# First attention of a graph network on one Trainium2 core: products three steps behind, one 138-column matmul for projection, scores and router

## The reference

```python
# first layer, attention (x: 8 x 1024 x 128, adj: 8 x 1024 x 1024 int32)
h = matmul(layernorm(x), W)
f1 = einsum('bnf,f->bn', h, a1); f2 = einsum('bnf,f->bn', h, a2)
e = leaky_relu(f1[:, :, None] + f2[:, None, :], negative_slope=0.2)
attention = softmax(where(adj > 0, e, -9e15), axis=1)
x = x + elu(matmul(attention, h))
# first layer, router of the experts (8 experts, 2 chosen)
z = layernorm(x)
mu, var = mean(z), mean(square(z - mu))
xn = (z - mu) * rsqrt(var + eps) * gamma + beta
logits = einsum('bsd,de->bse', xn, Wr) + br
top_vals, top_idx = top_k(logits, 2)        # softmax of these two are the shares
# then: experts on xn, second attention, second mixture of experts
```

## Time and profile before

| | |
|---|---|
| median of 3 runs | 1481.67 us (1479.19 to 1484.16) |
| the profiled execution's own time | 1483.64 us |
| its span, first to last instruction | 1481.9 us |
| TensorE busy | 1228.5 us, 83% |
| ScalarE, VectorE, GpSimd busy | 762.9, 655.1, 455.2 us |
| mean granted TensorE clock | 0.874 |
| product of the first attention (L539) | 256 rows, 168.1 us |
| `relu` (L631) waited for the logits | 114.9 us |

### The profile page before, as it was taken

How to read it: one execution, slowest core, us unless ns; L and a number is a source line. 1 busy time by engine, 2 the same in 40 slices (tenths; PEclk the granted TensorE clock), 3 DMA queues, 4 the chain that set the end, 5 groups by cost and what they waited for, 6 DMA issues and landing times. The chain is left out here.

```text
span 1481.9 us, 19195 instructions
## 1 busy us (share of the span) xinstructions
PE 1228.5 (83%) x5480; PEld 743.4 (50%) x5512; DVE 655.1 (44%) x2079; ACT 762.9 (51%) x1077; POOL 455.2 (31%) x519
## 2 busy tenths in 40 slices
PE   4988889788850899934687897799968999999998
PEld 3445445344430677722465675577754444444443
DVE  5565655656453233322454554465433422222222
ACT  4764663566530455512454464466643566656665
POOL 5133564553476112147414523532113200000000
PEclk8887787789775899976788998999985999999999
DMA  8832542441212344442212212211100000000000
GB/s 283 294 142 102 195 140 98 160 162 50 84 40 100 110 136 130 135 136 59 64 49 58 70 54 56 67 56 56 51 0 0 8 15 7 14 14 14 7 14 21
DMA packets 75543, 120.48 MB, mean 81 GB/s; under 512 B 8862, under 2 KB 49676, under 8 KB 74444
## 3 DMA queue, kind: packets, MB, share of 16 engines
q1 hardware_dynamic: 64156, 92.56, 19.1%
q0 software_dynamic: 11312, 27.02, 5.9%
HBM read 77.60 MB, written 41.94 MB: 81 GB/s over the span
## 5 line engine op out<-in xcount | busy, mean ns | idle before, releaser
L2097 DVE TENSOR_TENSOR dGW<-H,WBC 128x512 f32<-128x512 f32 x128 | 98.7, 771 | 231.6 <-ACT H L2065 230.8
L539 PE MATMUL O<-Y,HS 128*128 128x512 f32 x256 | 168.1, 792 | 15.0 <-DVE HS L790 14.9
L1746 DVE CUSTOM_DVE_ANT_0 f_Y<-f_T,f_R 128x1024 f32<-128x1024 f32 x64 | 78.4, 1225 | 197.3 <-ACT f_R L1699 160.8
L2065 ACT ACTIVATE H<-eU,bn 128x512 f32<-128x512 f32 x128 | 99.5, 777 | 114.9 <-PE eU L2009 114.8
L397 POOL DMA_INDIRECT sorted_x<-V,AT_I x128 | 124.6, 974 | 102.3 <-DVE AT_I L839 64.4
L1658 PEld LDWEIGHTS f_O<-f_XN,f_PT 128*128 128x128 f32 x1024 | 137.6, 211 | 35.9 <-issue 17.9
L1634 PE MATMUL f_T<-f_XT,f_XTA 128*128 128x512 f32 x256 | 137.7, 616 | 20.1 <-issue 13.7
L1658 PE MATMUL f_O<-f_XN,f_PT 128*128 128x128 f32 x1024 | 139.9, 295 | 12.4 <-ACT f_PT L1713 12.1
L631 ACT ACTIVATE R<-T,F 128x1024 f32<-128x1024 f32 x64 | 71.0, 1110 | 145.5 <-PE T L526 114.9
L1580 POOL DMA_INDIRECT W<-sorted_y,ROW_I x128 | 122.2, 955 | 42.8 <-issue 42.8
L2003 PE MATMUL eU<-XTN,V 128*128 (+1 forms) x256 | 132.5, 600 | 1.1 <-PEq L1879 1.1
(11 more groups left out here) (230 smaller groups left out, 1975.0 us busy)
## 6 DMA issues: line engine op xcount, KB each, us to landing
ADJ<-in_adj SPq DMA_DIRECT2D x64, 512.0 KB, 4.5
masks<-NM SPq DMA_DIRECT2D x8, 2048.0 KB
f_MK<-masks SPq DMA_DIRECT2D x64, 256.0 KB
XB<-sorted_x SPq DMA_DIRECT2D x39, 256.0 KB, 2.8
sorted_y<-YB POOLq DMA_DIRECT2D x39, 256.0 KB, 2.7
X<-in_x SPq DMA_DIRECT2D x8, 512.0 KB, 8.1
out_x<-X SPq DMA_DIRECT2D x16, 256.0 KB, 2.3
sorted_x<-zero SPq DMA_DIRECT2D x9, 256.0 KB
```

What stands on the lines that cost most here:

```text
L539: i = pe.matmul(O[:, h * HALF:(h + 1) * HALF], HS[:, g % 2, :], Y[:, g % 3, h * HALF:(h + 1) * HALF], start=False, stop=(c == NT - 1))
L1746: v.tensor_tensor_reduce(Y[:, g % 3, :], T[g % 2][:, :], R4[:, g % 2, :], -SLOPE, 3.0e38, ALU.add, ALU.min, LOW[:, g % RING:g % RING + 1]) ...
L2065: nc.scalar.activation(H2[:, s % 2, :], U2[s % 2][:, :], ACT.Relu, bias=bn[:, 3 * E + e:3 * E + e + 1], scale=bn[:, 2 * E + e:2 * E + e + ...
L2097: nc.vector.tensor_tensor(GW[:, s % 2, :], H2[:, s % 2, :], WBC[:, e, q * HALF:(q + 1) * HALF], ALU.mult).then_inc(gw_ready, 1)
```

## The change

- **One matmul for three results.** Wg is widened from 128 to 138 columns: the projection's weights, the two score vectors, and the router's weights scaled by gamma. `project` writes a tile's 138 columns, in three pieces of 3, 3 and 2 tiles (a PSUM bank holds three), and H keeps them all. `scores` is gone.
- **The router without transposes of its own.** The mean over features is taken out of the router's weights beforehand. The router is linear, so that its logits are the sum of two parts: that of the layer's input, which comes from the ten added columns times the row's deviation (XG), and that of the attention's ELU, a matmul with the transposes' source EL, which lies in SBUF already. `turn_r` and `copy_xr` are gone, `route` reads EL, and `choose` adds XG, multiplies by the root of the second norm (ROOT_R) and adds the bias.
- **Products three steps behind**, with Y in 4 buffers instead of 3, HS in 3 instead of 2.
- **Places of the extras.** `route` and `choose` of a sample stand at steps 5 and 7 of the next one, not at step 0 of the one after that; `rank` and `seat` at step 0, not 3; on TensorE an extra stands between a step's logits and its product, not behind the product. On GpSimd all 16 sends of a sample are one block ahead of the norms.
- Four loads more in the first stage (router weights, bias, gamma, beta), and two small matmuls ahead of the first transposes.

```diff
-        Wg = sb("Wg", [P, P])
-        WgT = sb("WgT", [P, 2])
+        WIDE = P + 2 + E
+        Wg = sb("Wg", [P, WIDE])
+        gb = sb("gb", [P, 2])
...
-                dve.wait_ge(gat_loaded, 32)
+                dve.wait_ge(gat_loaded, 96)
+                nc.vector.tensor_scalar(Wg[:, P + 2:WIDE], Wr0[:, :], gb[:, 0:1], None, ALU.mult).then_inc(gat_loaded, 1)
                 for k in range(2):
-                    nc.vector.tensor_tensor_reduce(products[:, :], Wg[:, :], A12[:, k * P:(k + 1) * P], 1.0, 0.0, ALU.mult,
-                                                   ALU.add, WgT[:, k:k + 1]).then_inc(gat_loaded, 1)
-                    dve.wait_ge(gat_loaded, 33 + k)
+                    nc.vector.tensor_tensor_reduce(products[:, :], Wg[:, 0:P], A12[:, k * P:(k + 1) * P], 1.0, 0.0, ALU.mult,
+                                                   ALU.add, Wg[:, P + k:P + k + 1]).then_inc(gat_loaded, 1)
+                    dve.wait_ge(gat_loaded, 98 + k)
...
+            THIRD = [(0, 3), (3, 6), (6, 8)]
+            MH = [M[0], M[1], M[0]]
...
-                def project(b, h):
-                    pe.wait_ge(xnt_ready[h], b + 1)
-                    for t in range(4 * h, 4 * h + 4):
-                        i = pe.matmul(M[h][:, t % 4 * P:(t % 4 + 1) * P], XNT[:, t * P:(t + 1) * P], Wg[:, :], start=True, stop=True)
-                    i.then_inc(h_ps[h], 1)
-
-                def scores(b):
-                    pe.wait_ge(h_ready[1], b + 1)
-                    for t in range(NT):
-                        i = pe.matmul(M[1][:, 2 * t:2 * t + 2], XNT[:, t * P:(t + 1) * P], WgT[:, :], start=True, stop=True)
-                    i.then_inc(f12_ps, 1)
+                def project(b, k):
+                    pe.wait_ge(xnt_ready[k > 0], b + 1)
+                    if k == 0:
+                        pe.wait_ge(xnt_ready[1], b + 1)
+                    elif k == 2:
+                        pe.wait_ge(h_ready[0], b + 1)
+                    first, end = THIRD[k]
+                    for t in range(first, end):
+                        i = pe.matmul(MH[k][:, (t - first) * WIDE:(t - first + 1) * WIDE], XNT[:, t * P:(t + 1) * P], Wg[:, :],
+                                      start=True, stop=True)
+                    i.then_inc(h_ps[k], 1)
...
                 def route(b):
-                    for h in range(2):
-                        pe.wait_ge(xrt_ready[h], b + 1)
+                    pe.wait_ge(x_added[0], b + 1)
                     for t in range(NT):
-                        i = pe.matmul(M[0][:, t * E:(t + 1) * E], XRT[:, t * P:(t + 1) * P], Wr0[:, :], start=True, stop=True)
+                        i = pe.matmul(M[0][:, t * E:(t + 1) * E], EL[:, t * P:(t + 1) * P], Wg[:, P + 2:WIDE], start=True, stop=True)
                     i.then_inc(lg_ps, 1)
...
+                pe.wait_ge(g_ready, 2)
+                pe.matmul(M[0][:, 0:E], XNT[:, 0:P], Wg[:, P + 2:WIDE], start=True, stop=True)
+                pe.matmul(M[0][:, E:2 * E], XNT[:, P:2 * P], Wr0[:, :], start=True, stop=True).then_inc(g_ps, 1)
+                pe.wait_ge(g_ready, 3)
...
+                for k in range(3):
+                    project(0, k)
                 turn_f1(0)
                 for g in range(G):
                     b, c = g // NT, g % NT
                     logits(g)
-                    if g >= 2:
-                        attend(g - 2)
                     if c == 0 and b >= 2:
-                        route(b - 2)
+                        pe.wait_ge(before_ready, 1)
+                        rank(b - 2)
                     if c == 1 and b < LAST:
                         for h in range(2):
                             turn_x(b + 1, h)
                     if c == 2 and b < LAST:
-                        for h in range(2):
-                            project(b + 1, h)
-                    if c == 3 and b >= 2:
-                        pe.wait_ge(before_ready, 1)
-                        rank(b - 2)
+                        for k in range(2):
+                            project(b + 1, k)
                     if c == 3 and b < LAST:
-                        scores(b + 1)
+                        project(b + 1, 2)
                     if c == 4 and b >= 1:
                         for h in range(2):
                             turn_el(b - 1, h)
                     if c == 5 and b < LAST:
                         turn_f1(b + 1)
-                    if c == 6 and b == 1:
-                        pe.wait_ge(x_added[0], 1)
+                    if c == 5 and b >= 1:
+                        route(b - 1)
+                    if c == 7 and b == 1:
+                        pe.wait_ge(f1r_ready, 3)
                         pe.wait_ge(par_loaded, 16 * len(loads))
-                        pe.transpose(M[0][:, 0:R], prow[:, :], ident[0:R, 0:R]).then_inc(pcol_ps, 1)
-                    if c == 7 and b >= 1:
-                        for h in range(2):
-                            turn_r(b - 1, h)
-                attend(G - 2)
-                route(LAST - 1)
-                attend(G - 1)
+                        pe.transpose(M[1][:, 0:R], prow[:, :], ident[0:R, 0:R]).then_inc(pcol_ps, 1)
+                    if g >= 3:
+                        attend(g - 3)
                 rank(LAST - 1)
+                for g in range(G - 3, G):
...
-                    if c == 0 and b >= 2:
-                        for h in range(2):
-                            copy_xr(b - 2, h)
+                    if c == 3 and b >= 1:
+                        grown(b - 1)
                     relu(g)
                     if g >= 1:
                         prob(g - 1)
-                    if c == 1 and b >= 1:
-                        grown(b - 1)
-                    if c == 2 and b < LAST:
+                    if c == 0 and b >= 2:
+                        weight(b - 2)
+                    if c == 0 and b >= 1:
+                        look(b, 3)
+                    if c == 1 and b < LAST:
                         for h in range(2):
                             copy_xnt(b + 1, h)
+                    if c == 2 and b < LAST:
+                        for k in range(2):
+                            copy_h(b + 1, k)
                     if c == 3 and b < LAST:
-                        for h in range(2):
-                            copy_h(b + 1, h)
-                    if c == 3 and b >= 2:
-                        weight(b - 2)
-                    if c >= 4 and b < LAST:
-                        look(b + 1, c - 4)
-                for h in range(2):
-                    copy_xr(LAST - 1, h)
+                        copy_h(b + 1, 2)
+                    if c in (4, 5, 7) and b < LAST:
+                        look(b + 1, (4, 5, 7).index(c))
...
-                    w = M[1][:, 0:2 * NT].rearrange("p (t k) -> p t k", k=2)
-                    op(v.tensor_copy, F3[:, :, 0], w[:, :, 0])
-                    op(v.tensor_tensor, FR[:, :], w[:, :, 0], F3[:, :, 0], ALU.subtract)
+                    q = b % 2
+                    op(v.tensor_copy, F3[:, :, 0], H[:, q, :, P])
+                    op(v.tensor_tensor, FR[:, :], H[:, q, :, P], F3[:, :, 0], ALU.subtract)
                     op(v.tensor_copy, F3[:, :, 1], FR[:, :])
                     v.tensor_tensor(F3[:, :, 2], FR[:, :], F3[:, :, 1], ALU.subtract)
                     if b >= 2:
                         dve.wait_ge(r4_ready, (b - 1) * NT)
-                    v.tensor_scalar(F2[:, b % 2, :], w[:, :, 1], 4.0, None, ALU.mult).then_inc(f2_ready, 1)
+                    v.tensor_scalar(F2[:, q, :], H[:, q, :, P + 1], 4.0, None, ALU.mult).then_inc(f2_ready, 1)
+                    op(v.tensor_tensor, STD[:, :], SPREAD[:, q, :], ROOT[:, q, :], ALU.mult)
+                    v.tensor_tensor(XG[:, b % 3, :, :], H[:, q, :, P + 2:WIDE], wide(STD[:, :]), ALU.mult)
...
-                    v.tensor_tensor(LG[:, :, :], M[0][:, 0:NT * E].rearrange("p (t e) -> p t e", e=E),
-                                    br0[:, :].unsqueeze(1).to_broadcast([P, NT, E]), ALU.add).then_inc(lg_read, 1)
+                    v.tensor_tensor(LG[:, :, :], M[0][:, 0:NT * E].rearrange("p (t e) -> p t e", e=E), XG[:, b % 3, :, :], ALU.add
+                                    ).then_inc(lg_read, 1)
                     dve.wait_ge(lg_read, b + 1)
+                    dve.wait_ge(root_ready, b + 1)
+                    op(v.tensor_tensor, LG[:, :, :], LG[:, :, :], wide(ROOT_R[:, b % 2, :]), ALU.mult)
+                    op(v.tensor_tensor, LG[:, :, :], LG[:, :, :], br0[:, :].unsqueeze(1).to_broadcast([P, NT, E]), ALU.add)
...
-                    if c == 2 and b >= 1:
+                    if c == 3 and b >= 1:
                         elu(b - 1)
                     shift(g)
                     if g >= 1:
                         share(g - 1)
                     if c == 0 and b >= 2:
-                        choose(b - 2)
+                        seat(b - 2)
                     if c == 1 and b + 2 < B:
                         if b == 0:
```

(49 more changed lines are left out.)

134 lines of the change are left out of this document (55 added, 79 removed).

## The result

| | us, median | runs | range |
|---|---|---|---|
| before | 1480.66 | 20 | 1472.95 to 1486.44 |
| changed | 1492.74 | 20 | 1479.50 to 1501.51 |

The changed kernel takes 1.0077 of the time before, 95% interval 1.0055 to 1.0099: 0.8% slower and clear of the noise, where 1425 was forecast. The ratios in this document are of undisturbed executions: one execution of changed_again, a run further down, took 2394 us, where its five others took 1349 to 1356, and is in none of them. Its profiled execution took 1488.69 us (span 1486.9, granted clock 0.867).

The account below looks back on a forecast made before the run. TensorE was taken as the bound, 52.2 us a sample: some 34 work, 8.3 idle, 9.9 lost to the clock. Savings of 48.0 (six samples), 2.5 (first) and 6 (drain) made 56.5, giving 1425 us, range 1398 to 1458.

Parts of the forecast that it names:

- Period 44.5: First attention, per sample: 31.4 us work, 6.5 idle, 6.6 lost to the clock; 8.0 under 52.5, 48.0 over six samples.
- Its idle part, 6.5: TensorE's idle time per sample: 4.3 for the ranking, 1.9 at the start of O, 0.3 for the router.
- GpSimd: the sixteen sends are one block ahead of the norms ... hidden: GpSimd, first attention: about 33 us work in 44 per sample; the norm is ready with 4 us to spare.
- The ranking waits 4.3: TensorE, step 0: the ranking waits 4.3 us for choose, moved to step 7; 0.8 as the other end.
- The start of O, "1.9, as now": TensorE's wait before a sample's output sum, for VectorE's ELU: kept at 1.9 us a sample.
- First sample, 2.5 gained: First sample, without routing or ranking, loses only the scores and their wait: 2.5 us less.
- The drain, 6 (2 to 9): After the last logits: last samples seated earlier, VectorE's tables end 6 us earlier, between 2 and 9.
- Rival D: Slower through GpSimd's block of sends if their pitch doubles to 2.5 us (threshold 2.4): about 1525 us; chance 0.07.
- Rival B: Choose on VectorE, held by norms, adds 4.3 us to the ranking's wait: 1451; or idle and clock unchanged: 1456; chance 0.22.
- C: The clock holds: drops halve, cost 3.5 us, period 41, total 1404 us; chance 0.14.
- E: No change: the wait moves and the period stays at 51 to 52 us; chance 0.05.
- no row of before shows whether VectorE is slowed in return: GpSimd's norm took 5.34 us beside VectorE's work, 3.44 with little; the reverse slowing was called unseen, since choose ran beside sends only.

Follow-up runs that it names:

- changed_again: The changed kernel word for word, on a chip where before takes 1384 us: 1351.89 us against 1387.99, ratio 0.975.
- masks_first: Changed kernel, but VectorE converts the next sample's last two mask tiles before the choice in step 7, not behind it: 0.976 of before.
- both edits: Changed kernel with the last mask tiles converted before the choice and the sends split as seven, normalization, nine: 0.966 of before.
- split_sends: Changed kernel, but GpSimd's sixteen sends go as seven, a normalization, then nine: 0.969 of before, 0.975 when run once more.
- paced_sends: Changed kernel, but sends spread three a step over steps 1 to 6, each group behind a wait for that step's ReLU: 0.976 of before.
- before_one_block: Kernel before, but a sample's sixteen sends in one row instead of nine and seven with a normalization between: 1.003 of before.
- both_2: Changed kernel with masks first and sends split, again, on a chip with late signals: 0.989 of before; its last two loop samples have unparted rows of sends.

## Why the prediction was wrong

- Period 44.5, the term that carried 48 of the 56.5 us: failed. Its busy part held, 38.0 forecast, 38.4 on a prompt chip; 40.1 on the late one, where the granted clock was 0.76 in the stretch instead of 0.82 (I had named 0.84 to 0.86). Its idle part, 6.5, was 7.9 and 13.7.
- The step that failed worst is "GpSimd: the sixteen sends are one block ahead of the norms ... hidden". I priced what GpSimd's own work takes, and its pitch (1.26 us) and row (20.1 us) came so, but I put at nothing what such a row does to other engines' signals. On the late chip ScalarE's "remote" waits are 49.4 us in five samples, and the late kind costs the changed kernel 44.7 us in six. The trace of before had the sign: signals up to 3.0 us late at ten of its twelve rows of 9 and 11 us, among them that of the earlier trace rows, where I took the ReLU's 1.11 us and passed over its "2.23 <-remote"; and gaps I read as waits for VectorE: on the prompt chip the product's wait for HS is 3.5 us instead of 10.3, and it is the ELU's that stayed, 8.5.
- "The ranking waits 4.3": the price was nearly right (3.4 in masks_first), the order wrong. I followed the choice to the ranking and not to what stands behind the choice on VectorE, two converts that the logits of step 0 need first. The wait was 5.4 to 6.1.
- The start of O, "1.9, as now": 1.1 on the prompt chip, 6.1 on the late one.
- First sample, 2.5 gained: none on the prompt chip (O of sample 1 at 80.9 against 80.8), 3.7 lost on the late one. The drain, 6 (2 to 9): 8.1 and 1.9.
- The sum against a prompt chip: 27.7 - 0.2 + 8.1 = 35.6 us of the forecast 56.5, ratio 0.975 instead of 0.962. With masks first and sends spaced it is 0.965 there, period 44.0.
- Rival D named the right place, the block of sends, with the wrong mechanism: its pitch stayed at 1.26 where 2.4 was needed. Rival B: the choice's 128x64 row took 294 ns in the mean in the changed kernel on the prompt chip, 224 with both edits, so VectorE is held a little:

```profile
L688 DVE TENSOR_TENSOR LG<-LG,br 128x64 f32<-128x64 f32 x5 | 1.5, 294 | 0.2
```
```profile
L690 DVE TENSOR_TENSOR LG<-LG,br 128x64 f32<-128x64 f32 x5 | 1.1, 224 | 0.2
```

The mean mixes two cases. Where GpSimd's norm ran beside it (152.53 us) the row took 0.40, where not (200.60) 0.23:

```profile
149.30 4.00 POOL L392 TENSOR_SCALAR V<-X,LESS_R,ROOT_R 128x128 f32<-128x128 f32 x7
...
152.53 0.40 DVE L688 TENSOR_TENSOR LG<-LG,br 128x64 f32<-128x64 f32 x1
...
200.60 0.23 DVE L688 TENSOR_TENSOR LG<-LG,br 128x64 f32<-128x64 f32 x1
```

That agrees with the Trainium skill, SBUF — State Buffer, "Who interferes with whom": the row reads two tiles of SBUF. HS reads one tile and one value a row, so that rule does not cover its 2.46 us. The whole choice took 3.98 us without a norm beside it (forecast 4.0) and 4.61 at most with one: 0.6 us a sample, where rival B had 4.3. The late chip had the norm beside the choice in four of its five samples, which is about the 0.7 us by which the mask wait is longer there. C and E did not occur.

The prediction says that no row of before shows whether VectorE is slowed in return. The trace did show it. One HS a sample stood beside the norm of the routing rows there, and in five samples it took 0.43 us instead of 0.29:

```profile
213.34 3.01 POOL L387 TENSOR_SCALAR V<-X,LESS_R,ROOT_R 128x128 f32<-128x128 f32 x6
```
```profile
215.14 0.43 DVE L790 TENSOR_SCALAR HS<-H,RZ 128x128 f32<-128x128 f32 x1
```

What stays open:

- The sends alone were never varied on a chip with late signals: split_sends, paced_sends and before_one_block all met prompt chips, and the runs on late chips that part the sends have masks first or another order of VectorE with it. That the long row of sends took the gain rests on the same kernel on both kinds of chip, on both_2's two kinds of rows, and on the gathers.
- With masks first and sends spaced the period is still 46.3 to 47.4 on late chips against 44.0 on a prompt one.
- Why the idle time kept to 6.5 to 8 us a sample on prompt chips through every order of choice and converts I tried.

## What to carry to other kernels

When a change joins short rows of software DMAs into a long one, look in the trace of before at the other engines' signals around the rows that are there, and keep rows to four or so: on prompt chips it cost nothing measurable, and on a late one it took 5% off the kernel, by one stage alone. When an operation moves on an in-order engine, price what is queued behind it, not only who waits for it. A ratio holds for the chip it was measured on, so the kernel before and its profile belong in every comparison.

## What the runs showed of the hardware

- Two kinds of chip, same kernel: before took 1478 to 1487 us in four of eight sets of runs and 1383 to 1388 in the other four. Only one chip had two sets, both prompt, so that the kind is the chip's own, and not that of the hour or the machine around it, is not shown. Of the 97 us between the profiled executions, 89 lie in the second attention, whose gathers stand in rows of sixteen and more; the last stages take the same time on both.
- On the late kind TensorE's signals come up to 15 us late within and behind a row of GpSimd's software DMAs, by the row's length: at most 1.5 us at four in a row, 3.7 at seven, 6 at eight and nine (at some of these rows none), 5 and 9 at the two rows of thirteen, 8 to 15 at sixteen. Where TensorE had little to do, in the first row of the second attention and in the rows of 10 to 15 of the drain, it was 2.4 at most. ScalarE's signals were never late in the two first profiles; VectorE's were by up to 2.3 us.
- There the trace itself holds fewer signals: 9,136 against 12,709 for the kernel before, most of them DMAs'. The page's row of the mask write shows it, on the late and on the prompt kind:

```profile
masks<-NM SPq DMA_DIRECT2D x8, 2048.0 KB
```
```profile
masks<-NM SPq DMA_DIRECT2D x8, 2048.0 KB, 11.7
```

Missing records and late signals may have one cause in how the events are recorded. The Trainium skill, NOTIFIC — Programmer's Manual, "2.4 When the ring fills", names three settings for a full queue of records: it drops the new ones, overwrites the oldest, or blocks the engine. Dropped ones fit the missing signals; whether blocking explains the lateness no run here shows, since every timed run was a profiled one, and a run without recording was not made.
